# Attention and MoE kernel: slot table by indirect writes, skewed units, seven PSUM banks

## What is computed

```python
h = tok(x)                       # state-space sum: 2*Re(sum_n Cm[c,h,n] * exp(K[h,n,l])), (8, 256, 512)
h = concatenate([h, txt], 1)     # (8, 384, 512), 3072 rows of 512
h = h + attn(layernorm(h))       # latent 128, compressed 64, causal softmax, 8 sequences of 384
h = h + ffn(layernorm(h))        # shared FFN of width 704, and 2 of 8 experts of width 352 for each row
```

## Time and profile before

| | us |
|---|---|
| median of 3 runs | 974.26 (972.4 to 977.86) |
| the profiled execution's own time | 966.46 |
| its span, first to last instruction | 964.6 |
| PE busy | 829.0 (86%) |
| DVE, ACT, POOL busy | 513.3, 395.0, 349.4 |
| mean granted TensorE clock | 0.967 of full |

### The profile page before, as it was taken

How to read it: one execution, slowest core, us unless ns; L and a number is a source line. 1 busy time by engine, 2 the same in 40 slices (tenths; PEclk the granted TensorE clock), 3 DMA queues, 4 the chain that set the end, 5 groups by cost and what they waited for, 6 DMA issues and landing times.

```text
span 964.6 us, 20136 instructions
## 1 busy us (share of the span) xinstructions
PE 829.0 (86%) x7301; PEld 522.5 (54%) x7302; DVE 513.3 (53%) x919; ACT 395.0 (41%) x683; POOL 349.4 (36%) x352
## 2 busy tenths in 40 slices
PE   0009999989799999699859997999999999999993
PEld 0009997655355545355436553666666666666661
DVE  7997746656652544736776442455434444444441
ACT  5863324334223232537442153454444444444441
POOL 0056744413810011524331032344444444444442
PEclk9999999989989999999979998999999999999996
DMA  5021234044412003597342054354444544444542
GB/s 191 0 66 47 59 111 143 24 88 121 111 45 66 1 24 108 135 225 160 92 90 80 23 153 155 79 89 83 83 79 85 87 87 76 79 85 86 87 76 33
DMA packets 66046, 84.68 MB, mean 88 GB/s; under 512 B 36096, under 2 KB 36224, under 8 KB 65344
## 3 DMA queue, kind: packets, MB, share of 16 engines
q0 software_dynamic: 12480, 29.37, 17.4%
q1 hardware_dynamic: 41408, 31.48, 11.8%
q10 hardware_dynamic: 12096, 22.94, 8.7%
HBM read 48.38 MB, written 27.53 MB: 79 GB/s over the span
## 4 chain that ended last, share of the span: by engine, by line
PE 72%; DVE 12%; ACT 6%; POOL 3%; issue 3%; DMA 2%; ACTq 0%; DVEq 0%; POOLq 0%
PE PS L2087 10%; PE PS L2089 10%; PE PS L2088 10%; PE PS L1075 7%; PE PS L590 6%; PE PS L1076 6%; PE PS L1077 6%; PE PS L2097 3%; PE PS L746 2%; PE PS L2119 2%; PE PS L1276 2%; PE PS L1233 1%; PE PS L2028 1%; DVE work L1422 1%; PE PS L1234 1%
## 5 line engine op out<-in xcount | busy, mean ns | idle before, releaser
L2087 PE MATMUL PS<-big,work 128*128 x605 | 200.9, 332 | 4.1 <-ACT work L2165 2.4
L2089 PE MATMUL PS<-big,work 128*128 x605 | 201.2, 333 | 0.0
L2088 PE MATMUL PS<-big,work 128*128 x605 | 201.2, 332 | 0.0
L2274 POOL DMA_INDIRECT out_dram<-work x55 | 88.0, 1600 | 62.5 <-DVE work L2244 46.0
L2206 DVE SCALAR_TENSOR_TENSOR work<-work,PS 128x352 f32<-128x352 f32 x55 | 28.7, 522 | 154.0 <-PE PS L2089 154.0
L2165 ACT ACTIVATE work<-PS 128x1024 f16<-128x1024 f16 x55 | 56.3, 1024 | 85.2 <-PE PS L2097 85.2
L2087 PEld LDWEIGHTS PS<-big,work 128*128 128x128 f16 x605 | 59.3, 98 | 42.6 <-issue 6.7
L2089 PEld LDWEIGHTS PS<-big,work 128*128 128x128 f16 x605 | 59.4, 98 | 42.2 <-issue 0.3
L2088 PEld LDWEIGHTS PS<-big,work 128*128 128x128 f16 x605 | 59.2, 98 | 36.5 <-issue 0.3
L994 POOL TENSOR_TENSOR big<-work,big 128x544 f16<-128x544 f32 (+1 forms) x30 | 38.0, 1267 | 108.8 <-ACT work L980 108.8
L2261 POOL DMA_INDIRECT big<-x_dram,work x55 | 55.8, 1015 | 46.7 <-POOL work L2258 45.0
(11 more groups left out here) (284 smaller groups left out, 1754.2 us busy)
## 6 DMA issues: line engine op xcount, KB each, us to landing
work<-in_weights ACTq DMA_DIRECT2D x36, 272.0 KB, 2.8
work<-in_shared ACTq DMA_DIRECT2D x28, 256.0 KB, 3.3
x_dram<-big SPq DMA_DIRECT2D x24, 256.0 KB, 2.3
out_dram<-big SPq DMA_DIRECT2D x24, 256.0 KB, 3.5
big<-in_weights ACTq DMA_DIRECT2D x20, 272.0 KB, 2.9
big<-in_weights SPq DMA_DIRECT2D x1, 2176.0 KB, 9.8
big<-in_par SPq DMA_DIRECT2D x1, 1185.0 KB, 10.7
big<-in_c_real SPq DMA_DIRECT2D x1, 1024.0 KB, 5.8
```

Of the source, the lines that this page charges most:

```text
L2087: pe.matmul(out, x_high, w_high, start=start, stop=False)
L2088: pe.matmul(out, x_high, w_low, start=False, stop=False)
L2089: return pe.matmul(out, x_low, w_high, start=False, stop=stop)
L2274: pool.indirect_dma_start(out_d, bass.IndirectOffsetOnAxis(ap=S_NUM[u][:, 0:1], axis=0), YO[u], None, compute_op=ALU.add).then_inc(s_add, 16)
```

## The change

- **Order of units** (`UNITS`): a block's first gate unit stands ahead of the previous block's three down units. Positions are 0 to 111; `after(b, u)` gives the count at which a unit is done. Blocks' rows are loaded and logits taken accordingly.
- **Banks**: units 46 to 105 rotate over banks 0 to 6.
- **Low halves** of all weight pieces are made by DVE; ACT's rescaling and `ON_POOL` go. Eight late pieces are split during units 14 to 40; the others follow a table by unit (`LATE_COUNT`): one or two with gate and down units, none in units 45 to 52 and 61 to 67, six from unit 98 on.
- **Rows** of pairs 2 and 3 are normed one at a time between units. POOL's bias additions for pairs 2 and 3 stand behind both halves of pair 1's rows and wait for unit 14; those for pair 1 stand behind the first half of pair 0.
- **Router**: steps start after unit 59 (were after 63); `count` stands before unit 70 (was 74); the slot offsets are done behind unit 72.
- **Slot table**: masks, `make_table` and `route_add` go. `slots_dram` is filled with padding at the start; POOL writes each of the 48 columns of 128 (row number, weight) pairs by an indirect DMA, two at a time from unit 74 on, then waits for all and loads `SLOTS` back.

```diff
 SH_UNITS = MCH + 3
+UNITS = [(b, u) for b in range(B) for u in range(SH_UNITS)]
+for b in range(1, B):
+    UNITS[SH_UNITS * b - 3:SH_UNITS * b + 1] = [(b, 0)] + [(b - 1, u) for u in range(MCH, SH_UNITS)]
 GATE_UNITS, UP_UNITS, HALF_M = (0, 2, 4, 5, 7, 9), (1, 3, 4, 6, 8, 10), 2
 SHARED_BLOCK = 2
 LAST_BLOCK = SHARED_BLOCK + 1
 NINE_FROM = 3
+
+
+def after(b, u):
+
+    return UNITS.index((b, u)) + 1
 
...
-        SPLITS = SHARED_PIECES + PIECES * len(LATE_BLOCKS)
-        FIRST_OF = {block: SHARED_PIECES + PIECES * k for k, block in enumerate(LATE_BLOCKS)}
+        LATE_PIECES = [(block, k) for block in (1, 6, 4, 5, 7) for k in range(PIECES)]
+        LATE_PIECES += [(8, k) for k in range(3)] + [(0, k) for k in range(PIECES)] + [(8, k) for k in range(3, PIECES)]
+        LAST_FROM = LATE_PIECES.index((0, 0))
+        SPLITS = SHARED_PIECES + len(LATE_PIECES)
+        LATE_COUNT = [0] * (B * SH_UNITS)
+        for n in range(43, B * SH_UNITS):
+            u = UNITS[n][1]
+            if n == B * SH_UNITS - 1:
+                count_here = 0
+            elif u >= MCH:
+                count_here = 2
+            else:
+                count_here = int(n in (73, 74, 76, 78, 80, 87, 88) or u in GATE_UNITS and u not in UP_UNITS and not 45 < n < 52 and not 60 < n < 68)
+            if n < 98:
+                LATE_COUNT[n] = min(count_here, LATE_PIECES.index((8, 3)) - PIECES - sum(LATE_COUNT))
+            else:
+                LATE_COUNT[n] = min(int(n in (98, 102, 103, 105, 107, 109)), len(LATE_PIECES) - PIECES - sum(LATE_COUNT))
+        assert sum(LATE_COUNT) == len(LATE_PIECES) - PIECES
+
+        def late_of(n):
+            first = SHARED_PIECES + PIECES + sum(LATE_COUNT[:n])
+            return range(first, first + LATE_COUNT[n])
+
+        FIRST_OF = {block: SHARED_PIECES + LATE_PIECES.index((block, 0)) for block in (0, 1, 4, 5, 6, 7, 8)}
...
         def low_done(eng, q):
-
-            if q in ON_POOL:
-                eng.wait_ge(sp_low_g, ON_POOL.index(q) + 1)
-            else:
-                eng.wait_ge(sp_low_v, q + 1 - sum(k < q for k in ON_POOL))
-
-        def lows_done(eng):
-            eng.wait_ge(sp_low_v, SPLITS - len(ON_POOL))
-            eng.wait_ge(sp_low_g, len(ON_POOL))
+            eng.wait_ge(sp_low, q + 1)
...
 
 
         def bank_of(n):
-            return 4 + n % 3
+            return (n - LATE_FROM) % 7 if LATE_FROM <= n < LATE_TO else 4 + n % 3
 
         def passes(pe, out, a_high, a_low, b_high, b_low, start, stop):
 
@@ -1076,11 +1103,19 @@
             pe.matmul(out, a_high, b_low, start=False, stop=False)
             return pe.matmul(out, a_low, b_high, start=False, stop=stop)
 
+        LATE_FROM, LATE_TO = 46, 106
+        BANKS = [bank_of(n) for n in range(B * SH_UNITS)]
+
         def bank_free(pe, n):
 
-            if n < 0:
+            earlier = [k for k in range(n) if BANKS[k] == BANKS[n]]
+            if not earlier:
+                if n >= LATE_FROM:
+                    pe.wait_ge(oa_v.sem, oa_v.at(f"h5_{PAIRS - 1}"))
+                    pe.wait_ge(at_a.sem, at_a.at(f"oT{PAIRS - 1}"))
                 return
-            b, u = divmod(n, SH_UNITS)
+            n = earlier[-1]
+            b, u = UNITS[n]
             if u >= MCH:
                 pe.wait_ge(ff_add, b * 3 + u - MCH + 1)
             elif u in UP_UNITS:
@@ -1100,12 +1135,12 @@
 
         def ffn_tensor(pe, n0, n1):
             for n in range(n0, n1):
-                b, u = divmod(n, SH_UNITS)
+                b, u = UNITS[n]
                 if u == 0:
...
             pe.wait_ge(s_xt[1], 3 * 16 * 3)
-            logits(pe, 7, XT_SH[1])
-            ffn_tensor(pe, 64, 74)
+            logits(pe, 6, XT_SH[1])
+            ffn_tensor(pe, 58, 60)
+            pe.wait_ge(s_xt_look[1], 3 * 16)
+            logits(pe, 7, XT_LOOK[1])
+            ffn_tensor(pe, 60, 70)
             count(pe)
-            ffn_tensor(pe, 74, 80)
-            for q in range(TABLE_TURNS):
-                make_table(pe, q)
-                ffn_tensor(pe, 80 + 2 * q, 82 + 2 * q)
-            ffn_tensor(pe, 96, B * SH_UNITS)
+            ffn_tensor(pe, 70, 76)
+            ffn_tensor(pe, 76, B * SH_UNITS)
...
             read_logits(dve, 6)
-            ffn_split_vector(dve, 62, 64, q + 16)
+            ffn_split_vector(dve, 58, 60)
             read_logits(dve, 7)
             route_logits()
-            ffn_split_vector(dve, 64, 66, q + 18)
+            ffn_split_vector(dve, 60, 62)
             route_scores()
-            ffn_split_vector(dve, 66, 67, q + 20)
+            ffn_split_vector(dve, 62, 63)
             route_groups_1()
-            ffn_split_vector(dve, 67, 69, q + 21)
+            ffn_split_vector(dve, 63, 65)
             route_groups_2()
-            ffn_split_vector(dve, 69, 72, q + 23)
-            route_experts()
-            ffn_split_vector(dve, 72, 74, q + 26)
+            ffn_split_vector(dve, 65, 67)
+            route_experts_1()
+            ffn_split_vector(dve, 67, 69)
+            route_experts_2()
+            ffn_split_vector(dve, 69, 70)
             route_counts()
-            ffn_split_vector(dve, 74, 76, q + 28)
+            ffn_split_vector(dve, 70, 71)
             route_slots()
-            ffn_split_vector(dve, 76, 78, q + 30)
+            ffn_split_vector(dve, 71, 72)
             route_table()
-            ffn_split_vector(dve, 78, 80, q + 32)
+            ffn_split_vector(dve, 72, 73)
+            route_offsets()
+            ffn_split_vector(dve, 73, 82)
             for u in range(3):
                 dve.wait_ge(s_x2[u], B * 16)
-            route_masks(0)
-            for k in range(TABLE_TURNS):
-                if k + 1 < TABLE_TURNS:
-                    route_masks(k + 1)
-                route_add(k)
-                if k < 3:
-                    ffn_split_vector(dve, 80 + 2 * k, 82 + 2 * k, q + 34 + 2 * k)
-                else:
-                    ffn_vector(dve, 80 + 2 * k, 82 + 2 * k)
-            ffn_split_vector(dve, 96, 104, q + 40)
-            ffn_split_vector(dve, 104, 112, q + 48)
+            ffn_split_vector(dve, 82, 96)
+            ffn_split_vector(dve, 96, B * SH_UNITS)
 
...
+                        pool.wait_ge(ff_p, SH_UNITS + 1)
                         bias(pool, 2)
-                    if i == 1 and half == 1:
                         bias(pool, 3)
-                        c_scale(pool, 2, 2, PAIRS)
-            late = iter(ON_POOL[SHARED_PIECES - MCH:-6])
-            deviation(pool, 3, "a")
-            split_low_g(pool, next(late))
-            deviation(pool, 3, "b")
-            split_low_g(pool, next(late))
-            rows_low(pool, 18)
-            split_low_g(pool, next(late))
-            rows_low(pool, 21)
-            for q in late:
-                split_low_g(pool, q)
+            for half in range(2):
+                deviation(pool, 3, "ab"[half])
+                rows_low(pool, 18 + 3 * half)
+            for n in range(NT):
+                if n:
+                    pool.wait_ge(ff_p, WRITES_FROM + 4 * n // 3)
+                slot_writes(pool, 2 * n, 2 * n + 2)
+            pool.wait_ge(s_scat, 16 * 2 * NT)
+            pool.dma_start(SLOTS.rearrange("p t c -> p (t c)").bitcast(U32), slots_d.rearrange("(p t) c -> p (t c)", p=P)).then_inc(
+                s_slots, 16)
+        def slot_writes(pool, n0, n1):
+            for n in range(n0, n1):
+                if n == 0:
+                    pool.wait_ge(s_slots0, 16)
+                    pool.wait_ge(ro_v.sem, ro_v.at("w1"))
+                k, t = divmod(n, NT)
+                pool.indirect_dma_start(slots_d, bass.IndirectOffsetOnAxis(ap=IDX[:, k, t:t + 1], axis=0),
+                                        PAY[:, n, :].bitcast(U32), None).then_inc(s_scat, 16)
 
         def q_scalar(act, i):
             act.wait_ge(at_p.sem, at_p.at(f"ct{i}"))
@@ -1667,14 +1737,15 @@
...
             nc.vector.tensor_scalar(SLT, SLT, MAGIC, None, ALU.subtract).then_inc(did("t3"), 1)
             own()
-            nc.vector.scalar_tensor_tensor(SL, SLT, -float(P), SL, ALU.mult, ALU.add).then_inc(did("row"), 1)
+            nc.vector.tensor_scalar(SL, SL, float(SLOT_TILES), None, ALU.mult).then_inc(did("i56"), 1)
+            own()
+            nc.vector.scalar_tensor_tensor(IDX, SLT, 1.0 - P * SLOT_TILES, SL, ALU.mult, ALU.add).then_inc(did("idx"), 1)
             for k in range(2):
+                nc.vector.tensor_copy(PAY[:, k * NT:(k + 1) * NT, 0].bitcast(U32), lc("token")).then_inc(did(f"tok{k}"), 1)
+            for k, m in enumerate((M0, M1)):
                 own()
-                nc.vector.tensor_tensor(TOKV[:, k, :], lc("token"), SL[:, k, :], ALU.subtract).then_inc(did(f"tok{k}"), 1)
+                nc.vector.tensor_copy(PAY[:, k * NT:(k + 1) * NT, 1], m).then_inc(did(f"w{k}"), 1)
+
...
-
-        def flat(x):
-            return x.rearrange("p k t -> p (k t)")
-
-        def route_masks(q):
-
-            u, cols = q % 2, slice(q * NCOL, (q + 1) * NCOL)
```

(16 more changed lines are left out.)

388 lines of the change are left out of this document (209 added, 179 removed).

## The result

| | before | after |
|---|---|---|
| median | 973.33 (4 runs, 971.7 to 977.9) | 912.08 (4 runs, 909.4 to 919.6) |
| profiled execution, span | 966.46, 964.6 | 909.40, 907.6 |
| PE busy | 829.0 (86%) | 805.6 (89%) |
| mean granted clock | 0.967 | 0.982 |

The ratio is 0.9376, with a 95% interval of 0.9312 to 0.944: faster by 6.2%, or 61.3 us at the medians and 57.1 between the two profiled executions.

What follows compares the result with a forecast made beforehand. PE was taken as the bound, losing time in waits for DVE. Gains of 12 + 33.4 + 8.5 + 1.5 = 55.4 us less 7.8 left net 47.6; 974.3 - 47.6 = 926.7 us, range 916 to 947.

Steps and rivals of the forecast that it cites:

- The bound and the places: PE bounds the middle (attention, shared FFN) and loses time in large waits, all on DVE, 33.4 us together.
- The table: Slot table in the shared FFN: eight turns of six matmuls leave PE, 1.49 us each at full clock; 12 us gained.
- Waits and clock: PE's waits for DVE in the middle, 33.4 us, and half clock in five windows behind them, 8.5 us, would go.
- The end of the middle: PE's wait before the first turn of x, behind the shared FFN, would go: 1.5 us.
- POOL's order: Pairs 1 to 3: moving bias additions ends DVE's lateness for the 7.2 us of bank waits; 2 us left standing.
- left standing or new 1 + 2 + 1 + 0.5 + 3.3 = 7.8: Deductions in the middle: down units 1, bias additions 2, router 1, pair 3 0.5, new stops of unknown place 3.3 us.
- The writes: POOL's 48 indirect writes from unit 74 on: 1.2 us each, hidden up to 1.65 each, cost 0.
- Rival A: Writes come late: at 2.0 us each PE waits 17 us before the routed loop; 946 us, chance 0.10.
- C: DVE and POOL lock each other during the writes, 3.2 us each, table 74 us late; 1001 us, chance 0.04.
- D: Another wait than DVE's holds PE at the same places, so nothing comes of it; about 972 us, chance 0.02.
- Rival B: Waits move to pieces ahead of multiplications in units 71 to 80; 21 us of gains come back; 948 us, chance 0.10.
- The signs named: Middle: PE busy 12 to 22 us less, end near 545, waits under 3, writes under 1.65, clock near 1.00 from 240.

Runs made afterwards that it cites:

- a_turns: Changed kernel with the table's eight turns of six f32 matmuls put back on PE, results not used: 921.35 us, ratio 0.9482 to before.
- b_bias: Kernel before with only POOL's bias additions moved to where the change puts them: 962.83 us, ratio 0.9919 to before.
- a_unpaced: Changed kernel without the waits for units between the pairs of indirect writes: 911.20 us, ratio 0.9393 to before.
- a_lowtwice_2: Repeat, beside the changed kernel on the same chip, of that kernel with each late low half made twice on DVE: 925.28 us, ratio 0.9537 to before.
- b_lowdve: Kernel before with 31 late low halves made by DVE instead of POOL, and ACT's rescaling copies for them gone: 964.98 us, ratio 0.9936 to before.
- a_banks3: Changed kernel with three banks for all units, no rotation over seven from unit 46 on: 917.74 us, ratio 0.9464 to before.
- a_again2: Changed kernel as it is, measured and profiled again: 911.52 us, ratio 0.9378 to before.
- a_lowtwice: Changed kernel with each of the 56 late pieces' low halves made twice on DVE: 925.24 us, ratio 0.9545 to before.
- a_thick2: Changed kernel with weight pieces also at gate units 61 to 67: 923.93 us, ratio 0.9537 to before.
- a_start: Changed kernel with ACT's copies of pair 1 ahead of piece 9 and POOL's pair 1 additions behind both halves of pair 0: 911.26 us.
- a_warm: Changed kernel with 10 unused identity products on PE, 6 ahead of pair 1's scores and 4 in their middle: 917.02 us, ratio 0.9461 to before.

## Why the prediction was right or wrong

**The bound and the places: right.** PE was held by five late meetings with DVE; four went, and the fifth shrank to 0.5 us, as forecast.

**The table: a little less than 12.** a_turns gives 10.6 us in the stretch and 8.5 at the medians. The term started from a turn's modelled length of 1.49; from start to start it is 1.32.

**Waits and clock: right.** From unit 46 on, the sum had 12 for the table, 23.8 for the waits (9.9, 9.4 and 4.5) and about 6 of the 8.5 for the clock (four of the five windows), some 42 in all ahead of any deduction. Measured are 44.3: 10.6 for the table, 25.1 of waits (with two small ones, 0.8 and 0.5, that the sum didn't count), and 8.6 left for the clock.

**The end of the middle: right,** 1.5 us of wait gone.

**POOL's order: right in the kernel before** (b_bias, 7.7 us), where the sum had 5.2 and the clock. In the changed kernel it is worth some 2, by the stretch from unit 8 to unit 30. DVE's operations beside the twelve additions are as long as the forecast feared (1.2 to 1.6 us at 267 to 277, where the shortest of their shapes take 0.55 to 0.71), but PE doesn't wait for them here; in a_unpaced and a_lowtwice_2 a stop of 1.4 us stands there.

**The step that failed is the line "left standing or new 1 + 2 + 1 + 0.5 + 3.3 = 7.8".** Next to none of it is there: 0 us of idle PE in the stretch, 1.3 in the rest of the middle. The largest item was the 3.3 for stops "without knowing where", on the ground that 38 more operations stand in DVE's in-order queue. That count is wrong by the change's own description: 46 low halves come, but each of the eight turns takes off four masks and an addition. DVE has 399 operations in the middle for 390, and from unit 46 on 205 for 214. b_lowdve shows what was missed besides: the low halves came from POOL, where they had made some of DVE's operations beside them two to four times as long. 31 of them cost DVE 7.5 us in place of 22.3, and the kernel got faster by 5.6 with no other edit than these and their copies on ACT. The forecast counted DVE at 228 us in the middle; it is 201. Some 13 of the 27 us are masks and additions that it didn't count off (26.9 us in the trace of before, where it took 14); the rest, some 15, is this relief. The forecast had the row for it (1003 ns for 167) and the rule, and used them for the bias additions alone. The other part is the banks: a_banks3 brings back 5.3 us of just such stops, at the places where the text expected them. a_lowtwice_2 shows that the caution wasn't empty, with 13.8 us for 40 us of DVE.

**The range failed by one more step, from the profile to the median.** Its low end, 916, was "all stops gone and no new ones", which is nearly what happened: with the 57.1 us between the two profiles the forecast's own conversion gives 974.3 - 57.1 = 917.2, inside the range. What lies below it comes from the conversion: the profile of before was 7.8 us under its median, that of after 2.7 under its own. I carried the 7.8 over as if it belonged to the kernel. It belongs to the runs: the three profiles of the changed kernel differ by up to 7.9 us in span, of which 6.4 arise before unit 46, in stops and half clock of another length each time. Of the kernel before, 7 of its 48 other executions lie at 964.8 to 967.3 us like the profiled one, most of the others at 970 to 974. A gain read from one profile carries an uncertainty of that size, and the range had none for it.

**The writes: right.** 1.27 us from start to start (1.32 in the mean) for 1.2, hidden, threshold 1.62 for 1.65. Rival A (2.0 us), C (3.2) and D have no sign. Rival B (pieces ahead of multiplications between units 71 and 80) doesn't come in the change, but with three banks it is what a_banks3 shows at unit 76, at a tenth of its price.

**The signs named:** PE busy 12 to 22 us less (20.4), no wait over 3 us (0.8 in this profile, though 3.2 at L1311 in a_again2's), no write over 1.65 (1.51), first gather 4 us early (13): as said. Middle near 545: 538.5. Clock near 1.00 from 240 on: yes.

## What to carry to other kernels

When work moves from GpSimd to VectorE, count not only what VectorE gets, but what its other instructions give back: look in the trace for operations of one shape with two lengths (0.36 and 1.38 us), and see what GpSimd did beside the long ones. Compare kernels by a stretch in which both do the same work, from one named instruction to another: here it repeats to 0.01 us while spans of the same kernel differ by 8. That holds where PE never waits in it; with waits it can differ too (a_lowtwice and its repetition by 2.8 us, a_thick2 and its by 8.1). And a sum of many operations goes by their mean, not their median. And deduct for unknown stops only where a place can be named whose cover is short; the cover is the peak in a few units, not the average.

## What was not expected of the hardware

- An indirect write of 128 rows of 8 bytes to DRAM is issued in 0.96 us (952 to 1506 ns), an accumulating scatter of 128 rows in 1.60, and a gather in 1.01; the writes follow each other every 1.27 us in the median and 1.32 in the mean.
- Two DVE operations of 0.36 us took 0.87 and 1.38 beside two subtractions of POOL of 1.2 to 1.4 us.
- The same program, profiled three times, had one and the same wait (for L1451, near 240) 0.8 to 3.2 us long, with 3.4 to 7 us at 1.2 GHz behind it, and ran at 2.4 GHz without a break from unit 46 to unit 111 each time.
- In four profiles taken together (a_start, a_warm, a_thick2, a_lowtwice) DVE stood still behind unit 80 for up to 7.5 us at a time (1.7 in a_lowtwice), released by nothing that the profile names; the cause is open.
